# Correlation products on two 64-column tiles of the array, and a band of six image rows in place of eight

## The chip, the cores and the metric

The kernel runs on 1 core of one Trainium2 chip. The metric is the device time of one execution in microseconds (us), the median of several runs. The engines are named as in the profile: PE is TensorE's matmul (PEld its weight loads), DVE is VectorE, ACT is ScalarE, POOL is GpSimd, and SP is SyncE, which here only issues DMAs.

## What is computed

Two layers follow each other, each on 8 images of 512 channels and 32x32 pixels. A layer normalises the image by groups of channels, takes the 25 correlations of each pixel with its 5x5 neighbours over the channels (of vectors scaled to length one), puts these 25 beside the 512 channels, multiplies by a 512x537 matrix, adds a bias, clips at zero, and adds the result to the image.

```
norm = jnp.sqrt(jnp.sum(feature * feature, axis=1, keepdims=True))
fn = feature / jnp.maximum(norm, EPS)
fp = jnp.pad(fn, ((0, 0), (0, 0), (PAD, PAD), (PAD, PAD)))
for cc in range(CS):
    for r in range(CS):
        sims.append(jnp.sum(fp[:, :, r:h + r, cc:w + cc] * fn, axis=1))
...
out = jnp.einsum('bihw,oi->bohw', x, conv_w) + conv_b[None, :, None, None]
...
x = x + _L0_conv_ref(_gn(x), L0_conv_conv_w, L0_conv_conv_b)
x = x + _L1_conv_ref(_gn(x), L1_conv_conv_w, L1_conv_conv_b)
```

## The kernel before

**Units and slots.** One image of one layer is a unit; there are 16, numbered k = 0 to 15. The images stay in SBUF between the layers (a ring of five in `xs`). Each engine has its program written out by hand, and semaphores join them. From unit 3 on the programs run in slots, one for each unit: slot k begins when TensorE starts the correlation products of unit k. Behind them come eight groups of 12 or 13 large matmuls (`channels`, L530, and `volume`, L539) of the units k-2 and k-1. So a unit's correlations are made one slot before its large matmuls need them.

**The way of a unit's correlations.**

1. TensorE multiplies the normalised image with itself (`products`, L470). The weights are 4 image rows (128 pixels, all 128 columns of the array), and the 8 rows around them pass as 256 columns (192 at the upper and lower edge, where rows are missing). Four channel tiles and two precision parts make 8 matmuls for one block of 128 pixels, 64 in all. Two blocks share one PSUM bank. The sum of a pixel's products with its neighbours then lies in a band along the diagonal.
2. ScalarE copies each bank to SBUF, four times for a unit (`band_out_of_psum`, L643), and SP writes each copy to a DRAM scratch (`band_through_dram`, L340).
3. SP waits until all four have landed, and issues two reads (`skew<-band_dram`, L346). Their row step in DRAM is one element more than a row's length, so that each pixel's own neighbours land at the same place of every partition.
4. VectorE takes lengths and scales (`neighbours`, L832 to L852); ScalarE gives a square root in between (`lengths`, L648).
5. TensorE transposes the result (`turn`, L520), at group 6 of the eight. The groups 6 and 7 stand behind it in TensorE's program, and then the next unit's products.
6. ScalarE copies it out (L654), SP writes it to DRAM (`rows_to_dram`, L356 and L358), and GpSimd's queue reads seven shifted views of it (L267 to L277; in units 0 and 1 SP's queue does). VectorE makes the 25 correlations in the next slot (`correlation`), and GpSimd's queue puts them in place (L286) for `volume`.

**What waits in order.** Every engine works through its own program in order. On VectorE `neighbours` stands behind the additions of the groups 0 and 1, and before those of the groups 2 to 7 and the statistics of unit k+2. On ScalarE `lengths` stands before the clipping of group 2. On SP the writes of results (`tiles_out`, L323) stand around the band's, and in the slots 6 to 8 the loads of the next images (`tiles_in`, L331) follow, before `rows_to_dram`. `gram_ps` has two banks, `conv_ps` four, `act_out` two buffers.

Of the kernel before, what the change touches and what calls it, by code (L numbers as in the profile page):

```python
# [25 lines left out]
ACT = mybir.ActivationFunctionType  # L26
# [5 lines left out]
P = 128  # L32
HALF = 512
# [24 lines left out]
def build(nc, x, w0, b0, w1, b1, out):  # L58
# [10 lines left out]
    BAND = (ROWS + 2 * R) * WI  # L69
# [23 lines left out]
    GSZ = GPAD + BLOCKS * P * BAND + GPAD  # L93
    GROUPS = 2 * KT
    BN = 6
    assert (B, UNITS) == (BATCHES, B * LAYERS) and BAND * 2 == HALF
# [7 lines left out]
    with ctx:  # L104
# [22 lines left out]
        band = sb("band", [P, PAIRS, HALF], F32)  # L127
# [76 lines left out]
        CONSTS = 11  # L204
# [95 lines left out]
        def _(sp):  # L300
# [9 lines left out]
            def pads():  # L310
                sp.wait_ge(const_step, CONSTS)
                for q in range(2):
                    sp.dma_start(band_dram[q:q + 1, 0:GPAD], rows[0:1, 0:GPAD]).then_inc(pads_out, 16)
                    sp.dma_start(band_dram[q:q + 1, GSZ - GPAD:GSZ], rows[0:1, 0:GPAD]).then_inc(pads_out, 16)
# [18 lines left out]
            def band_through_dram(k):  # L333

                q = k % 2
                for p in range(PAIRS):
                    sp.wait_ge(band_sb, PAIRS * k + p + 1)
                    dst = bass.AP(band_dram, q * GSZ + GPAD + 2 * p * P * BAND,
                                  [[BAND, P], [P * BAND, 2], [1, BAND]])
                    sp.dma_start(dst, band[:, p, :].rearrange("p (a n) -> p a n", a=2)).then_inc(band_out, 16)  # L340
                sp.wait_ge(band_out, 16 * PAIRS * (k + 1))
                wait(sp, rn_step, RN_STEPS * k)
                for h in range(HALVES):
                    src = bass.AP(band_dram, q * GSZ + GPAD - R + h * FOLD * P * BAND,
                                  [[BAND + 1, P], [P * BAND, FOLD], [1, REACH]])
# [46 lines left out]
        def _(pool):  # L392
# [14 lines left out]
            pool.memset(band[:, 0, 0:R * WI], 0.0).then_inc(const_step, 1)  # L407
            pool.memset(band[:, PAIRS - 1, HALF - R * WI:HALF], 0.0).then_inc(const_step, 1)
# [44 lines left out]
        def _(pe):  # L453
# [10 lines left out]
            def product(u, j, t, part):  # L464

                p, h = j // 2, j % 2
                r0 = max(ROWS * j - R, 0)
                r1 = min(ROWS * (j + 1) + R, HI)
                at = h * BAND + (r0 - (ROWS * j - R)) * WI
                return pe.matmul(gram_at(u, p)[:, at:at + (r1 - r0) * WI],  # L470
                                 opnd[:, u % RING, 0, t, j * P:(j + 1) * P],
                                 opnd[:, u % RING, part, t, r0 * WI:r1 * WI],
                                 start=(t == 0 and part == 0 and (u > 0 or h == 0)),
                                 stop=(t == KT - 1 and part == 1 and (u > 0 or h == 1)))

            def first_products():

                for t in range(KT):
                    pe.wait_ge(high, t + 1)
                    pe.wait_ge(low, t + 1)  # L480
                    for p in range(PAIRS):
                        for j in (2 * p, 2 * p + 1):
# [507 lines left out]
```

## Time and profile before

| | |
|---|---|
| time, median of 3 runs | 539.54 us (538.83 to 540.25) |
| the profiled execution: span | 538.4 us |
| PE busy | 490.8 us, 91% of the span |
| DVE busy | 350.5 us, 65% |
| ACT busy | 278.6 us, 52% |
| chain that ended last | PE 77%, DVE 10%, ACT 4%, DMA 4% |

The page and the views give times in us from the span's start. Busy time counts an engine's instructions; matmuls follow each other in a pipeline, so one matmul's own duration is longer than the step to the next one, and steps are read from starting times. The span runs from the first to the last instruction of the profiled execution. It lies 1.1 us below the median of the runs.

### The profile page before, as it was taken

How to read it: one execution, taken by the hardware profiler on the slowest of the kernel's cores; microseconds unless marked ns; L12 is line 12 of the kernel's file. 1: busy time of each engine (PE TensorE's matmuls, PEld its weight loads, DVE VectorE, ACT ScalarE, POOL GpSimd, SP SyncE). 2: the span in 40 equal slices, each digit the busy share in tenths (PEclk: the TensorE clock that was granted, in tenths of full speed). 3: DMA queues.
4: the chain of work that ended last, by engine and by line, in shares of the span. 5: the costliest groups of instructions: out<-in, count | busy, mean ns of one | idle time of the engine just before them, and what ended most of it. 6: DMA issues, size and time to landing. Idle time of an engine off the chain costs nothing.

```text
span 538.4 us, 7705 instructions
## 1 busy us (share of the span) xinstructions
PE 490.8 (91%) x2824; PEld 278.2 (52%) x2824; DVE 350.5 (65%) x820; ACT 278.6 (52%) x370; POOL 131.8 (24%) x189
## 2 busy tenths in 40 slices
PE   0658699489998999999999999999999999999996
PEld 0535355354644646464645556464646455564442
DVE  4788794767869296958758595858677676433322
ACT  1352544575394656647393757556473938433222
POOL 3453511040521313131220404040313112040400
PEclk9989799789999999999999999999999999999999
DMA  8282444441332716494957625042332326362332
GB/s 295 99 270 67 129 165 133 133 134 38 94 92 74 219 49 211 149 309 131 321 165 254 212 102 161 15 129 47 98 89 75 110 79 185 138 203 90 126 126 114
DMA packets 58547, 75.81 MB, mean 141 GB/s; under 512 B 11764, under 2 KB 45612, under 8 KB 58510
## 3 DMA queue, kind: packets, MB, share of 16 engines
q1 hardware_dynamic: 48718, 66.40, 36.7%
q0 software_dynamic: 9792, 8.92, 7.0%
q8 instruction: 22, 0.36, 0.3%
q14 instruction: 15, 0.12, 0.1%
HBM read 34.97 MB, written 37.79 MB: 135 GB/s over the span
## 4 chain that ended last, share of the span: by engine, by line
PE 77%; DVE 10%; ACT 4%; DMA 4%; POOL 2%; SPq 2%; issue 2%; DVEq 0%; ACTq 0%
PE conv_ps L530 56%; PE gram_ps L470 14%; PE conv_ps L539 5%; DVE stats L759 3%; POOL v L432 2%; DVE opnd L808 2%; DMA xs<-in_x_dram 1%; ACT opnd L627 1%; PE turn_ps L520 1%; ACT v L633 1%; DVE wmax L858 1%; ACT act_out L662 1%; DMA skew<-band_dram 1%; DMA band_dram<-band 1%; DVE xs L886 1%
## 5 line engine op out<-in xcount | busy, mean ns | idle before, releaser
L530 PE MATMUL conv_ps<-opnd,wh 128*128 128x512 f16 x512 | 194.9, 381 | 1.2 <-DVE wl L874 1.2
L530 PE MATMUL conv_ps<-opnd,whh 128*128 128x512 f16 x512 | 194.7, 380 | 0.0
L530 PE MATMUL conv_ps<-opnd,wl 128*128 128x512 f16 x512 | 194.7, 380 | 0.0
L662 ACT ACTIVATE act_out<-conv_ps,bias,wdown 128x512 f32<-128x512 f32 x128 | 96.4, 775 | 141.0 <-PE conv_ps L539 129.1
L886 DVE TENSOR_TENSOR xs<-xs,act_out 128x512 f32<-128x512 f32 x128 | 87.7, 696 | 50.8 <-ACT act_out L662 50.2
L470 PE MATMUL gram_ps<-opnd 128*128 128x256 f16 (+1 forms) x960 | 105.0, 269 | 3.4 <-ACT band L643 3.4
L470 PEld LDWEIGHTS gram_ps<-opnd 128*128 128x128 f16 x960 | 91.1, 100 | 16.6 <-ACT band L643 3.7
L808 DVE SCALAR_TENSOR_TENSOR opnd<-opnd,v 128x1024 f16<-128x1024 f16 x64 | 78.4, 1235 | 28.7 <-ACT v L633 21.3
L627 ACT ACTIVATE opnd<-xs,affine 128x1024 f16<-128x1024 f32 x64 | 78.8, 1238 | 17.4 <-DVE affine L802 17.4
L759 DVE BATCH_NORM_STATS2 stats<-xs 128x6 f32<-128x512 f32 x128 | 79.9, 681 | 5.6 <-DMA xs<-in_x_dram 5.6
L530 PEld LDWEIGHTS conv_ps<-opnd,whh 128*128 128x128 f16 x512 | 50.0, 98 | 61.2 <-issue 1.0
L530 PEld LDWEIGHTS conv_ps<-opnd,wh 128*128 128x128 f16 x512 | 50.2, 98 | 58.8 <-POOL whh L424 1.3
L530 PEld LDWEIGHTS conv_ps<-opnd,wl 128*128 128x128 f16 x512 | 50.2, 98 | 57.5 <-issue 0.8
L633 ACT ACTIVATE v<-xs,affine 128x1024 f32<-128x1024 f32 x52 | 64.4, 1238 | 6.1 <-DVE opnd L808 6.1
L267 POOL DMA_DIRECT2D mirror<-rows_dram x14 | 9.5, 678 | 232.0 <-DMA rows_dram<-rows 232.0
L286 POOL DMA_DIRECT2D vol<-corr_h x48 | 33.2, 697 | 105.7 <-DVE corr_h L825 105.6
L539 PE MATMUL conv_ps<-vol,wvol 96*128 96x512 f16 x128 | 47.2, 396 | 11.7 <-DMA vol<-corr_h 11.7
L643 ACT ACTIVATE band<-gram_ps 128x448 f32<-128x448 f32 (+1 forms) x60 | 32.5, 560 | 20.2 <-PE gram_ps L470 20.2
L817 DVE TENSOR_TENSOR mirror<-mirror,rn_own 100x256 f32<-100x256 f32 x16 | 6.8, 424 | 49.1 <-DMA rn_far<-rows_dram 49.1
L277 POOL DMA_DIRECT2D rn_far<-rows_dram x56 | 34.1, 744 | 0.0
L539 PEld LDWEIGHTS conv_ps<-vol,wvol 96*128 96x128 f16 x128 | 12.6, 100 | 27.6 <-DMA vol<-corr_h 12.3
L432 POOL TENSOR_SCALAR v<-xs,affine 128x1024 f32<-128x1024 f32 x12 | 21.7, 1817 | 18.5 <-DVE affine L802 11.8
(77 smaller groups left out, 238.6 us busy)
## 6 DMA issues: line engine op xcount, KB each, us to landing
xs<-in_x_dram SPq DMA_DIRECT2D x32, 512.0 KB, 6.4
band_dram<-band SPq DMA_DIRECT2D x64, 256.0 KB, 2.9
out_dram<-xs SPq DMA_DIRECT2D x32, 512.0 KB, 2.9
skew<-band_dram SPq DMA_DIRECT2D x32, 266.0 KB, 3.5
vol<-corr_h POOLq DMA_DIRECT2D x48, 50.0 KB, 2.7
rows_dram<-rows SPq DMA_DIRECT2D x32, 65.8 KB
rows_dram<-rows SPq DMA_DIRECT2D x32, 63.3 KB
mirror<-rows_dram POOLq DMA_DIRECT2D x14, 110.9 KB, 2.6
```

Of the source, the lines that this page charges most:

```text
L277: eng.dma_start(rn_far[c:QPARTS:QUARTERS, 0:run], bass.AP(rows_dram, rn_row + c * QRUN, [[1, S], [PW, S], [1, run]])).then_inc(arrived, 16)
L286: eng.dma_start(vol[at:at + NS, k % 2, :].rearrange("s (q n) -> s q n", q=QUARTERS), corr_h[:, part, :]).then_inc(vol_in, 16)
L470: return pe.matmul(gram_at(u, p)[:, at:at + (r1 - r0) * WI], opnd[:, u % RING, 0, t, j * P:(j + 1) * P], opnd[:, u % RING, part, t, r0 * W ...
L530: pe.matmul(conv_ps[:, g % 4, :], w[:, l, t, m * P:(m + 1) * P], opnd[:, u % RING, part, t, n * HALF:(n + 1) * HALF], start=(t == 0 and w ...
L539: pe.matmul(conv_ps[:, g % 4, :], wvol[0:96, l, m * P:(m + 1) * P], vol[0:96, u % 2, n * HALF:(n + 1) * HALF], start=False, stop=True).the ...
L627: act.activation(opnd[:, u % RING, 0, t, :], xs[:, ring_slot(unit_batch(u)), t, :], ACT.Identity, bias=affine[:, 0, 1, t:t + 1], scale=aff ...
L633: act.activation(v2[:, t % 2, :], xs[:, ring_slot(unit_batch(u)), t, :], ACT.Identity, bias=affine[:, 1, 1, t:t + 1], scale=affine[:, 1, 0 ...
L643: act.activation(band[:, p, a:z], gram_at(u, p)[:, a:z], ACT.Copy).then_inc(band_sb, 1)
L662: act.activation(act_out[:, g % 2, :], conv_ps[:, g % 4, :], ACT.Relu, bias=bias[:, l, m:m + 1], scale=wdown[:, l, m:m + 1]).then_inc(relu, 1)
L759: last = dve.bn_stats(stats[:, t, h, :], xs[:, ring_slot(b), t, h * HALF:(h + 1) * HALF])
L808: dve.scalar_tensor_tensor(out=opnd[:, u % RING, 1, t, :], in0=opnd[:, u % RING, 0, t, :], scalar=-2.0, in1=v2[:, t % 2, :], op0=ALU.mult, ...
L886: dve.tensor_tensor(xt, xt, act_out[:, g % 2, :], ALU.add).then_inc(x_sum, 1)
```

## The change

The weights of one correlation matmul become 2 image rows (64 pixels) in place of 4, and 6 rows pass (192 columns) in place of 8. A block of 128 pixels is now made by two such matmuls, one on the array's columns 0 to 63 and one on the columns 64 to 127, in turn: for each channel tile and part first one half (`s` = 0), then the other. At the image's upper and lower edge a matmul of 64 columns fills the places of rows that are missing (`filler`). A bank holds the blocks p and p+4 in place of 2p and 2p+1.

The band is 192 columns wide in place of 256. ScalarE copies 384 columns of each bank. The DMA to DRAM writes each tile of 64 pixels in one piece, with a gap of 64 elements between tiles, and its destination has three steps (2 tiles, 64 pixels, 384 elements) in place of (128 pixels, 2 blocks, 256 elements). The reads keep their size and take another start and step. The two fills of the band's edges with zeros on GpSimd go, and the gaps in DRAM are filled with zeros once.

```diff
--- before.py
+++ after.py
@@ -66,7 +66,11 @@
     GROUP = C // 32
     ROWS = P // WI
     BLOCKS = PIX // P
-    BAND = (ROWS + 2 * R) * WI
+    TROWS = 2
+    TILE = TROWS * WI
+    SPLIT = P // TILE
+    BAND = (TROWS + 2 * R) * WI
+    STEP = 2 * BAND + 1
     PAIRS = BLOCKS // 2
     REACH = 2 * R * WI + S
     CENTRE = R * WI + R
@@ -90,10 +94,10 @@
     A_PITCH = S * (B_PITCH + PW) - 1
     ROWS_SZ = (NS + 1) * PSZ + S * A_PITCH
     GPAD = 64
-    GSZ = GPAD + BLOCKS * P * BAND + GPAD
+    GSZ = GPAD + PAIRS * P * STEP
     GROUPS = 2 * KT
     BN = 6
-    assert (B, UNITS) == (BATCHES, B * LAYERS) and BAND * 2 == HALF
+    assert (B, UNITS) == (BATCHES, B * LAYERS) and BAND * 2 <= HALF and TILE <= GPAD
 
     weights = (w0, w1)
     biases = (b0, b1)
@@ -124,7 +128,7 @@
         wvol = sb("wvol", [P, LAYERS, C], F16)
         vol = sb("vol", [P, 2, PIX], F16)
         v2 = sb("v2", [P, 2, PIX], F32)
-        band = sb("band", [P, PAIRS, HALF], F32)
+        band = sb("band", [P, PAIRS, 2 * BAND], F32)
         skew = sb("skew", [P, BLOCKS, REACH], F32)
         nbr = sb("nbr", [P, BLOCKS, H_PART], F32)
         rows = sb("rows", [H_PART + NROWS, FRAME], F32)
@@ -201,7 +205,7 @@
         relu = sem("relu")
         x_sum = sem("x_sum")
 
-        CONSTS = 11
+        CONSTS = 9
         BN_STEPS = KT + KT + 2
         GN_STEPS = 11
         RN_STEPS = 8
@@ -311,7 +315,9 @@
                 sp.wait_ge(const_step, CONSTS)
                 for q in range(2):
                     sp.dma_start(band_dram[q:q + 1, 0:GPAD], rows[0:1, 0:GPAD]).then_inc(pads_out, 16)
-                    sp.dma_start(band_dram[q:q + 1, GSZ - GPAD:GSZ], rows[0:1, 0:GPAD]).then_inc(pads_out, 16)
+                    sp.dma_start(bass.AP(band_dram, q * GSZ + GPAD + TILE * 2 * BAND,
+                                         [[TILE * STEP, PAIRS * SPLIT], [1, TILE]]),
+                                 rows[0:PAIRS * SPLIT, 0:TILE]).then_inc(pads_out, 16)
                 sp.wait_ge(pads_out, 64)
 
             def tiles_out(u, tiles):
@@ -335,14 +341,14 @@
                 q = k % 2
                 for p in range(PAIRS):
                     sp.wait_ge(band_sb, PAIRS * k + p + 1)
-                    dst = bass.AP(band_dram, q * GSZ + GPAD + 2 * p * P * BAND,
-                                  [[BAND, P], [P * BAND, 2], [1, BAND]])
-                    sp.dma_start(dst, band[:, p, :].rearrange("p (a n) -> p a n", a=2)).then_inc(band_out, 16)
+                    dst = bass.AP(band_dram, q * GSZ + GPAD + p * P * STEP,
+                                  [[TILE * STEP, SPLIT], [2 * BAND, TILE], [1, 2 * BAND]])
+                    sp.dma_start(dst, band[:, p, :]).then_inc(band_out, 16)
                 sp.wait_ge(band_out, 16 * PAIRS * (k + 1))
                 wait(sp, rn_step, RN_STEPS * k)
                 for h in range(HALVES):
-                    src = bass.AP(band_dram, q * GSZ + GPAD - R + h * FOLD * P * BAND,
-                                  [[BAND + 1, P], [P * BAND, FOLD], [1, REACH]])
+                    src = bass.AP(band_dram, q * GSZ + GPAD - R + h * BAND,
+                                  [[STEP, P], [P * STEP, FOLD], [1, REACH]])
                     sp.dma_start(skew[:, h:BLOCKS:HALVES, :], src).then_inc(skew_in, 16)
 
             def rows_to_dram(k):
@@ -404,8 +410,6 @@
                                pattern=[[GROUP, P // GROUP], [0, GROUP]], channel_multiplier=-1
                                ).then_inc(const_step, 1)
             pool.memset(rows[:, :], 0.0).then_inc(const_step, 1)
-            pool.memset(band[:, 0, 0:R * WI], 0.0).then_inc(const_step, 1)
-            pool.memset(band[:, PAIRS - 1, HALF - R * WI:HALF], 0.0).then_inc(const_step, 1)
             pool.memset(vol[:, :, :], 0.0).then_inc(const_step, 1)
             pool.memset(wvol[:, :, :], 0.0).then_inc(const_step, 1)
             pool.memset(nbr[:, :, NROWS:H_PART], 0.0).then_inc(const_step, 1)
@@ -461,17 +465,39 @@
                 pe.matmul(turn_ps[:, 1, 0:2 * KT], avg[:, :], mv[:, :, :].rearrange("p t s -> p (t s)"),
                           start=True, stop=True).then_inc(group_avg, 1)
 
-            def product(u, j, t, part):
-
-                p, h = j // 2, j % 2
-                r0 = max(ROWS * j - R, 0)
-                r1 = min(ROWS * (j + 1) + R, HI)
-                at = h * BAND + (r0 - (ROWS * j - R)) * WI
-                return pe.matmul(gram_at(u, p)[:, at:at + (r1 - r0) * WI],
-                                 opnd[:, u % RING, 0, t, j * P:(j + 1) * P],
-                                 opnd[:, u % RING, part, t, r0 * WI:r1 * WI],
-                                 start=(t == 0 and part == 0 and (u > 0 or h == 0)),
-                                 stop=(t == KT - 1 and part == 1 and (u > 0 or h == 1)))
+            def off_image(j, s):
+
+                top = TROWS * (j * SPLIT + s) - R
+                return max(-top, 0) * WI, max(top + TROWS + 2 * R - HI, 0) * WI
+
+            def tile_at(u, j, s, first, size):
+
+                at = j // FOLD * BAND + first
+                return gram_at(u, j % FOLD)[s * TILE:(s + 1) * TILE, at:at + size]
+
+            def opens(u, j):
+
+                return u > 0 or j < FOLD
+
+            def filler(u, j, s):
+
+                above, below = off_image(j, s)
+                n, size = j * SPLIT + s, above + below
+                if size:
+                    pe.matmul(tile_at(u, j, s, 0 if above else BAND - below, size),
+                              opnd[:, u % RING, 0, 0, n * TILE:(n + 1) * TILE],
+                              opnd[:, u % RING, 0, 0, 0:size], start=opens(u, j), stop=False)
+
+            def product(u, j, s, t, part):
+
+                above, below = off_image(j, s)
+                n = j * SPLIT + s
+                first, size = (TROWS * n - R) * WI + above, BAND - above - below
+                return pe.matmul(tile_at(u, j, s, above, size),
+                                 opnd[:, u % RING, 0, t, n * TILE:(n + 1) * TILE],
+                                 opnd[:, u % RING, part, t, first:first + size],
+                                 start=(t == 0 and part == 0 and opens(u, j) and size == BAND),
+                                 stop=(t == KT - 1 and part == 1 and (u > 0 or j >= FOLD)))
 
             def first_products():
 
@@ -479,9 +505,13 @@
                     pe.wait_ge(high, t + 1)
                     pe.wait_ge(low, t + 1)
                     for p in range(PAIRS):
-                        for j in (2 * p, 2 * p + 1):
+                        for j in (p, p + FOLD):
+                            if t == 0:
+                                for s in range(SPLIT):
+                                    filler(0, j, s)
                             for part in range(2):
-                                last = product(0, j, t, part)
+                                for s in range(SPLIT):
+                                    last = product(0, j, s, t, part)
                         if t == KT - 1:
                             last.then_inc(gram, 1)
 
@@ -491,10 +521,13 @@
                     pe.wait_ge(high, KT * (u + 1))
                     pe.wait_ge(low, KT * (u + 1))
                 pe.wait_ge(band_sb, PAIRS * u + p - 1)
-                for j in (2 * p, 2 * p + 1):
+                for j in (p, p + FOLD):
+                    for s in range(SPLIT):
+                        filler(u, j, s)
                     for t in range(KT):
                         for part in range(2):
-                            last = product(u, j, t, part)
+                            for s in range(SPLIT):
+                                last = product(u, j, s, t, part)
                 last.then_inc(gram, 1)
 
             def turn_weights(l, n):
@@ -638,9 +671,7 @@
                 act.wait_ge(gram, PAIRS * u + p + 1)
                 if p == 0:
                     wait(act, band_out, 16 * PAIRS * u)
-                a = R * WI if p == 0 else 0
-                z = HALF - (R * WI if p == PAIRS - 1 else 0)
-                act.activation(band[:, p, a:z], gram_at(u, p)[:, a:z], ACT.Copy).then_inc(band_sb, 1)
+                act.activation(band[:, p, :], gram_at(u, p)[:, 0:2 * BAND], ACT.Copy).then_inc(band_sb, 1)
 
             def lengths(u):
```

On TensorE one half of the products of a unit from slot 3 on, and the beginning of the other, stand so before (`turn_ps<-mv,avg` is the group average of the next unit, in the middle of the products; the numbers behind a name are partitions and columns of the output):

```order
L470 MATMUL gram_ps<-opnd 128x192 x8
L470 MATMUL gram_ps<-opnd 128x256 x24
L461 MATMUL turn_ps<-mv,avg 128x8
L470 MATMUL gram_ps<-opnd 128x256 x24
L470 MATMUL gram_ps<-opnd 128x192 x8
```

And around the same average in the changed program, to the beginning of the last block (L487 is the filler):

```order
L496 MATMUL gram_ps<-opnd 64x128
L496 MATMUL gram_ps<-opnd 64x192 x49
L465 MATMUL turn_ps<-mv,avg 128x8
L496 MATMUL gram_ps<-opnd 64x192 x48
L487 MATMUL gram_ps<-opnd 64x64
L496 MATMUL gram_ps<-opnd 64x192
L496 MATMUL gram_ps<-opnd 64x128
```

Nothing has moved past the average; a unit has 128 products of half the weights' columns in place of 64, and two fillers.

On SP's queue the DMAs of unit 3 stand so before (the numbers are the steps' counts of the destination):

```order
L340 DMA band_dram<-band 128x2x256 x4
L346 DMA skew<-band_dram 128x4x133 x2
L356 DMA rows_dram<-rows 26x648
L358 DMA rows_dram<-rows 5x5x648
L356 DMA rows_dram<-rows 26x648
```

And in the changed program:

```order
L346 DMA band_dram<-band 2x64x384 x4
L352 DMA skew<-band_dram 128x4x133 x2
L362 DMA rows_dram<-rows 26x648
L364 DMA rows_dram<-rows 5x5x648
L362 DMA rows_dram<-rows 26x648
```

The order on SP is the same; the destination of the band's writes has 2 as its outermost count in place of 128.

## Rows read from the trace of the kernel before

**Rows 1.** The page: span, and busy time of each engine.
```profile
span 538.4 us, 7705 instructions
...
PE 490.8 (91%) x2824; PEld 278.2 (52%) x2824; DVE 350.5 (65%) x820; ACT 278.6 (52%) x370; POOL 131.8 (24%) x189
```

**Rows 2.** TensorE in slot 12, in order of time: start, duration, line.
```profile
381.48 3.44 PE L470 MATMUL gram_ps<-opnd 128*128 128x192 f16 x32
384.75 0.29 PE L461 MATMUL turn_ps<-mv,avg 128*128 128x8 f32 x2
...
405.03 0.60 PE L520 MATMUL turn_ps<-ident,nbr 128*115 128x128 f32 x4
...
411.09 1.15 PE L470 MATMUL gram_ps<-opnd 128*128 128x192 f16 x11
```

**Rows 3.** Line 470 alone, slot 12, eight matmuls: busy PE, PEld.
```profile
381.48:382.13 0.65, 0.65 (x8) 0.65 (x8) 1.00 0.00 0
```

**Rows 4.** SP's queue in slot 12, in order of time: issue, time it took, line.
```profile
383.78 6.38 SPq L340 DMA_DIRECT2D band_dram<-band  x4
392.19 0.92 SPq L346 DMA_DIRECT2D skew<-band_dram  x2
```

**Rows 5.** VectorE in slot 12, in order of time.
```profile
397.86 0.17 DVE L832 TENSOR_SCALAR nsq<-skew 128x8 f32<-128x8 f32 x1
...
400.13 0.91 DVE L852 TENSOR_TENSOR nbr<-skew,nbr 128x200 f32<-128x200 f32 x2
```

**Rows 6.** DMA issues by line, with median us to landing.
```profile
band_dram<-band SPq DMA_DIRECT2D x64, 256.0 KB, 2.9
...
skew<-band_dram SPq DMA_DIRECT2D x32, 266.0 KB, 3.5
```

**Rows 7.** DMA packets from 390.0 to 392.1: two band DMAs.
```profile
DMA packets 544, 0.52 MB, mean 250 GB/s; under 512 B 32, under 2 KB 544, under 8 KB 544
...
q1 hardware_dynamic: 544, 0.52, 73.0%
```

**Rows 8.** DMA packets from 380.2 to 381.7: one DMA of line 358.
```profile
DMA packets 31, 0.08 MB, mean 54 GB/s; under 512 B 5, under 2 KB 5, under 8 KB 30
...
q1 hardware_dynamic: 30, 0.06, 12.9%
```

**Rows 9.** DMA packets from 49 to 52: lines 267 to 277 on SP's queue.
```profile
q1 hardware_dynamic: 261, 0.29, 30.8%
...
rn_far<-rows_dram SPq DMA_DIRECT2D x4, 27.7 KB
```

**Rows 10.** DMA queues from 384.0 to 388.6: the views beside the band.
```profile
q0 software_dynamic: 364, 0.39, 37.3%
```

**Rows 11.** SP's queue in slots 7 and 8: loads of x, then the band.
```profile
255.72 2.91 SPq L331 DMA_DIRECT2D xs<-in_x_dram  x4
...
265.32 7.11 SPq L340 DMA_DIRECT2D band_dram<-band  x4
```

**Rows 12.** SP's queue in unit 0, in order of time.
```profile
26.88 1.98 SPq L340 DMA_DIRECT2D band_dram<-band  x4
31.35 0.91 SPq L346 DMA_DIRECT2D skew<-band_dram  x2
```

**Rows 13.** VectorE in unit 0, in order of time.
```profile
40.91 0.89 DVE L852 TENSOR_TENSOR nbr<-skew,nbr 128x200 f32<-128x200 f32 x2
```

**Rows 14.** TensorE, first products of slots 3, 4 and 5.
```profile
104.37 3.78 PE L470 MATMUL gram_ps<-opnd 128*128 128x192 f16 x32
...
138.46 3.44 PE L470 MATMUL gram_ps<-opnd 128*128 128x192 f16 x32
...
173.90 0.34 PE L470 MATMUL gram_ps<-opnd 128*128 128x192 f16 x2
```

**Rows 15.** Stretches: busy time, granted clock (PEclk), DMA share, GB/s.
```profile
56.90:61.70 4.80, 0.13 (x2) 0.04 (x1) 2.82 (x13) 2.36 (x4) 4.18 (x5) 0.89 0.31 87
61.80:65.20 3.40, 3.40 (x9) 1.16 (x10) 2.46 (x3) 2.78 (x4) 3.11 (x2) 0.50 0.29 89
```

## The prediction

> **What bounds the kernel now.** I began with the page: TensorE is busy for 490.8 of 538.4 us [rows 1], so a saving elsewhere gives nothing as long as nothing makes TensorE wait. Then I read one slot in order of time on each engine. Slot 12 takes 411.09 - 381.48 = 29.61 us [rows 2], without a gap on TensorE: 6.7 us of products, 16.9 us of groups 0 to 5, the turn at 405.03, which is 23.55 us after the slot's start (I write +23.55), and 6.06 us from there to the next slot. The reader is to see that the turn is the only place in a slot where TensorE depends on work of the same slot: the way products, copy, band to DRAM, skew, neighbours, turn. That way has slack. SP issues the first band write at +2.30 and the skew reads at +10.71 [rows 4]; neighbours ends at 401.04, +19.56 [rows 5], 4.0 us before the turn. The first operation on the skew starts at 397.86, +16.38; the reads, issued within 0.92 us and landing in 3.5 us [rows 4, 6], are there at about +14.5, so VectorE came 1.9 us later than it might have. All in all the band may land some 5.9 us later before TensorE waits.
>
> **The products.** Of the first 32, eight pass 192 columns at 81 ns each [rows 3]; the other 24 fill the rest of 3.27 us [rows 2], 109 ns each. The trace has no matmul on half of the array. If the two halves run side by side, a pair costs one passage of 192 columns, 81 ns: 64 pairs make 5.2 us, with fillers and changes between whole and half array perhaps 5.4, a gain of 1.3 us a slot. If they run one behind the other, a pair costs 162 ns and the products 10.4 us, a loss of 3.7 us. If weight loads were not covered either, a load of about 81 ns, the second figure of [rows 3], on each gives 324 ns a pair and 20.7 us. I take the middle of the first two, no difference in the products' length, because the term that follows hides both ends: TensorE reaches the turn at +22.3 or +27.3, and either is too early. The end of the first quarter, which starts the band, moves by -0.3 to +1.0 us; I take 0.
>
> The Trainium skill, TensorEngine Tiling (Array Packing), section Theoretical Speedup, gives up to 2x for such tiles, but its section Restrictions says that column tiling turns the fast weight load off. By the first the products would take about 5.2 us and by the second the loads could be seen; no run here shows either yet.
>
> **The band's write to DRAM** is the term that I think decides. Its destination's outermost count was 128 and is now 2. The trace shows what that count does. Each DMA ends with one small packet on every engine that it used, and these are the packets under 512 B: two band writes of 128 leave 32, so 16 engines each [rows 7]; a DMA of line 358, with 5 outermost in DRAM, leaves 5 [rows 8]. The views on SP's queue, 25 outermost on their DRAM side or 5, keep 30.8% of 16 engines busy, 4.9 engines, and this although several of them are in the queue at once [rows 9]: DMAs behind each other use the same five, they do not take others. So I expect each band write on two engines, and all four of a unit on the same two.
>
> The Trainium skill, DMA: Bandwidth & Descriptors, section Why a DMA increments its semaphore by 16 and not by 1, states it as a rule: the largest number up to 16 that divides the outermost counts of both sides, on the lowest-numbered engines. The rows above agree (16 for 128, 5 for 5 and 25); by the rule the count here is 2.
>
> Price of a packet: 73.0% of 16 engines for 2.1 us over 512 packets of 1 KB is 48 ns [rows 7]; 12.9% for 1.5 us over 25 packets of 2592 B is 124 ns [rows 8]. Both are 47 to 48 ns per KB; the new packets of 1536 B come to 72 ns. These rows were taken with busy engines beside them, so I use 68 (bounds 60 and 80). One engine carries 64 packets of each write: 4.35 us, and 17.4 us for four (15.4 to 20.5). The copies come fast enough to keep the two busy. Before, a write of 256 KB took 2.9 us to landing [rows 6], of which 256 packets on 16 engines are 0.8, so 2.1 us are fixed.
>
> New way in a slot: first issue +2.3, fixed part and transfers 2.1 + 17.4, landed at +21.8 (was +10.7); skew reads 3.8, +25.6; neighbours 2.5 without its wait for VectorE, +28.1. The views on GpSimd's queue run at the same time; they use 37.3% of 16 engines for 4.6 us [rows 10], 1.7 us on a mean engine, and I add 1.0 for what falls on the two. So the turn comes at +29.1, not at +23.55: 5.5 us later (2.5 to 9).
>
> **The clock.** TensorE then waits about 5.6 us at each turn. In unit 0's wait before, 4.8 us nearly without matmuls were followed by 3.4 us at a granted 0.50, the level of 1.2 GHz [rows 15]. The 6.06 us behind a turn would run at that level for some part; I add 1.5 us (0 to 3.4). Together 7.0 us a slot. If the products run one behind the other, TensorE comes at +27.3, waits less and keeps its clock, but the band starts 1.0 us later: the sum stays about the same.
>
> **Which slots.** Slots 5 to 15 are eleven: 77 us. Slots 3 and 4 already take 34.1 and 35.4 us [rows 14], because second-layer weights are turned in them, and the new way needs 29.1 + 6.06 = 35.2: nothing more. In unit 0 the first write is issued at 26.88 and the skew at 31.35 [rows 12]; now the band lands at 26.88 + 19.5 = 46.4, the reads at 50.2, neighbours ends at 52.7 in place of 41.80 [rows 13]: 10.9 us, and TensorE has little to do meanwhile. Units 1 and 2 have more slack; 2 us each. Start: 15 us (10 to 22). In slots 7 to 9 the band's first write stands behind loads of x issued by the slot before (four of 512 KB [rows 11], 128 KB on each engine, some 6 us); SP now issues these loads later in the slot, since it waits for the band first, so they reach into the next. I add 2.7 us three times, 8 us (0 to 15).
>
> **Small edits.** ScalarE's copy of 384 columns in place of 512 and the two fills less on GpSimd shorten work that is not waited for: 0. The bytes to DRAM fall by a quarter, which would matter if 16 engines carried them. The skew reads keep their shape, 128 outermost: 0.
>
> **Sum.** 538.4 + 77 + 15 + 8 = 638.4 us of span; with the 1.1 us by which the median lies above the span, 639.5, so 640 us.
>
> **Rivals.**
> Faster: the write spreads over 16 engines after all, as every DMA of 128 partitions shows [rows 7], and the halves run side by side. Then the band lands no later than now, and 15 units gain 1.3 us each (unit 0 waits for its input): 520 us. Against it stand the five engines of [rows 8, 9]. What decides the sign then is a pair of products at 102 ns, the mean of 16 steps of 81 and 48 of 109 now.
> Slower, but otherwise: 16 engines, and the halves one behind the other: 15 x 3.7 = 56 us, 595 us.
> Two engines, but other two for each write: the last one lands about 3.6 us later than now, within the slack of 5.9, and the products decide: 520 or 595.
> Much slower: weight loads uncovered. A slot then takes 20.7 + 16.9 + 6.06 = 43.7 us, 14 more in 15 units: about 750 us.
>
> **Chances.** My forecast (two engines, band late at every turn) 0.82; spread and side by side 0.08; spread and serial 0.06; loads uncovered 0.04. Its own range adds the low bounds, 3 x 11 + 10 = 43 us, and the high ones within reason, 11 x 10.5 + 22 + 15 = 152 us: 582 to 692. I give 588 to 690, which holds most of it and the 595 case, some 8 in 10. A measurement of this kernel can tell about 0.3% from no change. Faster by more than that 0.07, within it 0.02, slower 0.91.
>
> **What would show it.** In the profile after: band writes with 4 packets under 512 B for two of them in place of 32; landing of the band, where it is told, several times 2.9 us; SP waiting for the band before the skew for some 14 us in a slot; TensorE idle before line 553, put down to VectorE's `nbr`; DMA share near 2/16 in the middle of a quiet slot; clock at 0.5 behind the turns. A pair of products at 81 or 162 ns shows the array's part. I am wrong if the band lands at its old place, if a turn starts at +24 or earlier, or if the packets take well under 60 ns.

## The result, and the profile after

The changed kernel takes 671.93 us (median of four runs, 670.90 to 672.83), the kernel before 539.89 us (four runs, 538.83 to 540.68). The ratio is 1.2451, with a 95% interval of 1.2428 to 1.2474: slower by almost a quarter. The profiled execution has a span of 671.0 us, 132.6 us more than before.

The page of the changed kernel: span, busy time, the chain of waits by engine and by line, and two groups of instructions with the idle time ahead of them.

```profile
span 671.0 us, 9815 instructions
...
PE 521.6 (78%) x3880; PEld 284.5 (42%) x3880; DVE 349.5 (52%) x820; ACT 274.0 (41%) x370; POOL 128.6 (19%) x187
...
DMA 43%; PE 30%; DVE 14%; ACT 5%; issue 4%; SPq 2%; POOL 1%; DVEq 0%; ACTq 0%
DMA band_dram<-band 34%; PE conv_ps L563 19%; DMA skew<-band_dram 8%; PE gram_ps L496 6%; DVE stats L790 3%; PE turn_ps L553 2%; ACT band L674 2%; ACT opnd L660 1%; DVE nbr L883 1%; SPq L346 1%; DVE xs L917 1%; PE conv_ps L572 1%; DVE opnd L839 1%; SPq L352 1%; DMA xs<-in_x_dram 1%
...
L553 PE MATMUL turn_ps<-ident,nbr 128*115 128x128 f32 x64 | 18.1, 434 | 90.6 <-DVE nbr L883 90.6
...
L863 DVE TENSOR_SCALAR nsq<-skew 128x8 f32<-128x8 f32 x16 | 2.8, 172 | 151.0 <-DMA skew<-band_dram 151.0
```

TensorE is busy 78% of the span in place of 91% [rows 1]. The chain now runs through DMAs for 43% of the time, 34% in the band's writes alone, and 90.6 us of TensorE's idle time stand ahead of one line, the turn. What makes the turn late is seen in slot 12, the slot that [rows 2, 4, 5] show of before. TensorE, in order of time:

```profile
483.27 2.83 PE L496 MATMUL gram_ps<-opnd 128*64 128x192 f16 x64
486.03 0.39 PE L465 MATMUL turn_ps<-mv,avg 128*128 128x8 f32 x2
486.35 2.47 PE L496 MATMUL gram_ps<-opnd 128*64 128x192 f16 x49
...
489.33 0.39 PE L563 MATMUL conv_ps<-opnd,wh 128*128 128x512 f16 x1
...
511.64 1.20 PE L553 MATMUL turn_ps<-ident,nbr 128*115 128x128 f32 x4 [5.28 <-DVE nbr L883]
520.15 0.22 PE L487 MATMUL gram_ps<-opnd 128*64 128x64 f16 x1
```

SP's queue in the same slot:

```profile
485.33 8.47 SPq L346 DMA_DIRECT2D band_dram<-band  x4
505.34 0.95 SPq L352 DMA_DIRECT2D skew<-band_dram  x2
```

And VectorE in that slot:

```profile
509.19 0.17 DVE L863 TENSOR_SCALAR nsq<-skew 128x8 f32<-128x8 f32 x1 [9.66 <-DMA skew<-band_dram]
...
510.69 0.90 DVE L883 TENSOR_TENSOR nbr<-skew,nbr 128x200 f32<-128x200 f32 x2
```

The products got shorter: from the slot's start to the average, 64 of them take 2.76 us where the first 32 of before took 3.27. The first band write is issued at +2.06 (before +2.30). Then SP waits, and the skew reads go out at +22.07, not +10.71; VectorE stands idle 9.66 us for them; neighbours ends at 511.59, +28.32; the turn comes at +28.37 after 5.28 us of waiting. From there to the next slot it is 8.51 us, before 6.06.

Why the band is late is in the DMA packets. From 493 to 497, when nothing but band writes is under way:

```profile
DMA packets 132, 0.20 MB, mean 50 GB/s; under 512 B 2, under 2 KB 132, under 8 KB 132
...
q1 hardware_dynamic: 132, 0.20, 13.2%
```

2 of 16 engines are 12.5%: two are busy and fourteen idle. 13.2% of 16 x 4 us over the 130 packets that are not small is 65 ns a packet of 1536 B. One write ended in this stretch and left two packets under 512 B, where 16 engines left 16 a write [rows 7].

The clock behind the turn of the same slot, as a whole and in its two parts (columns as in [rows 15]):

```profile
511.64:520.15 8.51, 8.51 (x30) 3.87 (x30) 8.51 (x14) 2.71 (x4) 0.28 (x1) 0.73 0.12 33
...
511.64:516.28 4.64, 4.64 (x13) 2.30 (x14) 4.64 (x8) 1.94 (x3) 0.00 (x0) 0.50 0.02 6
516.28:520.15 3.87, 3.87 (x18) 1.57 (x16) 3.87 (x8) 0.78 (x1) 0.28 (x1) 1.00 0.23 66
```

The whole stretch has the same work as the 6.06 us of before, at a mean granted clock of 0.73, after 5.28 us in which TensorE had nothing to do: 4.64 us at 0.50, the level of 1.2 GHz, and the rest at 1.00, that of 2.4 GHz.

The 132.6 us lie in three places, each measured by the first products of a slot. Slot 3 starts at 129.31 in place of 104.37 [rows 14]: 24.9 us. Slots 3 and 4 together take 17.9 us more (slot 5 starts at 216.69, before 173.90: 42.8 us, less 24.9). Slots 5 to 15, with the groups that follow the last of them, take the rest, 89.8 us. TensorE's first products of unit 2 and its turn, the first products of slot 3 and its turn, and those of slot 5:

```profile
90.66 5.33 PE L496 MATMUL gram_ps<-opnd 128*64 128x192 f16 x64
...
125.40 1.20 PE L553 MATMUL turn_ps<-ident,nbr 128*115 128x128 f32 x4 [7.19 <-DVE nbr L883]
129.31 5.07 PE L496 MATMUL gram_ps<-opnd 128*64 128x192 f16 x64
...
163.03 1.20 PE L553 MATMUL turn_ps<-ident,nbr 128*115 128x128 f32 x4 [4.17 <-DVE nbr L883]
...
216.69 0.22 PE L487 MATMUL gram_ps<-opnd 128*64 128x64 f16 x1
```

SP's first band write in units 2 and 3:

```profile
100.12 7.43 SPq L346 DMA_DIRECT2D band_dram<-band  x4
...
137.43 7.73 SPq L346 DMA_DIRECT2D band_dram<-band  x4
```

Slot 4 shows another wait than the turn's, here on TensorE:

```profile
193.99 0.38 PE L563 MATMUL conv_ps<-opnd,whh 128*128 128x512 f16 x1
203.38 0.87 PE L543 MATMUL gram_ps<-ident,xs 128*128 128x128 f32 x3 [9.01 <-DVE wl L905]
```

and on VectorE:

```profile
197.78 0.17 DVE L863 TENSOR_SCALAR nsq<-skew 128x8 f32<-128x8 f32 x1 [7.70 <-DMA skew<-band_dram]
...
202.56 0.68 DVE L905 TENSOR_TENSOR wl<-gram_ps,wh 128x512 f16<-128x512 f32 x1
```

The low parts of the second layer's weights (line 905) stand on VectorE behind the first operation on the skew. When the skew is late, they are late too, and TensorE's transposes of the next weights wait for them.

### The profile page after: what moved, and what is told of

Its sections match the earlier page's. It is cut to its first block, busy times and chain, and to the rows that moved or that the text cites. A ratio compares the mean times of both kernels' runs of the same rounds, so it can differ in the third digit from the quotient of the medians.

```text
span 671.0 us, 9815 instructions
## 1 busy us (share of the span) xinstructions
PE 521.6 (78%) x3880; PEld 284.5 (42%) x3880; DVE 349.5 (52%) x820; ACT 274.0 (41%) x370; POOL 128.6 (19%) x187
## 4 chain that ended last, share of the span: by engine, by line
DMA 43%; PE 30%; DVE 14%; ACT 5%; issue 4%; SPq 2%; POOL 1%; DVEq 0%; ACTq 0%
DMA band_dram<-band 34%; PE conv_ps L563 19%; DMA skew<-band_dram 8%; PE gram_ps L496 6%; DVE stats L790 3%; PE turn_ps L553 2%; ACT band L674 2%; ACT opnd L660 1%; DVE nbr L883 1%; SPq L346 1%; DVE xs L917 1%; PE conv_ps L572 1%; DVE opnd L839 1%; SPq L352 1%; DMA xs<-in_x_dram 1%
## 5 line engine op out<-in xcount | busy, mean ns | idle before, releaser
L563 PE MATMUL conv_ps<-opnd,wh 128*128 128x512 f16 x512 | 207.2, 405 | 1.4 <-ACT act_out L693 1.0
L563 PE MATMUL conv_ps<-opnd,wl 128*128 128x512 f16 x512 | 205.9, 402 | 0.0
L563 PE MATMUL conv_ps<-opnd,whh 128*128 128x512 f16 x512 | 204.5, 399 | 0.0
L496 PE MATMUL gram_ps<-opnd 128*64 128x192 f16 (+1 forms) x1920 | 92.7, 254 | 4.2 <-ACT band L674 3.8
L553 PE MATMUL turn_ps<-ident,nbr 128*115 128x128 f32 x64 | 18.1, 434 | 90.6 <-DVE nbr L883 90.6
L496 PEld LDWEIGHTS gram_ps<-opnd 128*64 128x64 f16 x1920 | 84.1, 115 | 7.2 <-ACT band L674 6.9
L563 PEld LDWEIGHTS conv_ps<-opnd,wh 128*128 128x128 f16 x512 | 53.0, 103 | 67.7 <-issue 12.0
L863 DVE TENSOR_SCALAR nsq<-skew 128x8 f32<-128x8 f32 x16 | 2.8, 172 | 151.0 <-DMA skew<-band_dram 151.0
L679 ACT ACTIVATE nrm<-nsq 128x8 f32<-128x8 f32 x16 | 3.3, 208 | 148.7 <-DVE nsq L863 148.7
L572 PE MATMUL conv_ps<-vol,wvol 96*128 96x512 f16 x128 | 47.3, 396 | 11.4 <-DMA vol<-corr_h 11.4
L553 PEld LDWEIGHTS turn_ps<-ident,nbr 128*115 128x115 f32 x64 | 13.4, 288 | 98.4 <-DVE nbr L883 98.4
```

The costliest lines, as they stand in the source:

```text
L496: return pe.matmul(tile_at(u, j, s, above, size), opnd[:, u % RING, 0, t, n * TILE:(n + 1) * TILE], opnd[:, u % RING, part, t, first:first ...
L553: last = pe.transpose(turn_ps[0:H_PART + NROWS, 0, i * P:(i + 1) * P], both[:, i, 0:H_PART + NROWS], ident[:, :])
L563: pe.matmul(conv_ps[:, g % 4, :], w[:, l, t, m * P:(m + 1) * P], opnd[:, u % RING, part, t, n * HALF:(n + 1) * HALF], start=(t == 0 and w ...
L572: pe.matmul(conv_ps[:, g % 4, :], wvol[0:96, l, m * P:(m + 1) * P], vol[0:96, u % 2, n * HALF:(n + 1) * HALF], start=False, stop=True).the ...
```

## Experiments

The theory after the result: the outermost count of the band write's destination puts the write on two engines, and all the loss follows from that. Rivals: the loss comes from the products on half the array, from the new layout in DRAM, or from the clock. The kernels with two writes a bank and with one row step ran four to six times; each of the others ran once. Runs of one kernel lie up to 4 us apart here, so a difference of 3 to 4 us between single runs is weak evidence.

**Two writes a bank.** The same layout and products; only the outermost count becomes 64.

```diff
-dst = bass.AP(band_dram, q*GSZ + GPAD + p*P*STEP, [[TILE*STEP, SPLIT], [2*BAND, TILE], [1, 2*BAND]])
-sp.dma_start(dst, band[:, p, :])
+for s in range(SPLIT):
+    dst = bass.AP(band_dram, q*GSZ + GPAD + (p*P + s*TILE)*STEP, [[2*BAND, TILE], [1, 2*BAND]])
+    sp.dma_start(dst, band[s*TILE:(s + 1)*TILE, p, :])
```

> The changed kernel, but each bank's copy is written to DRAM by two DMAs, one for each tile of 64 pixels, so that 64 stands outermost and not 2; products, band and reads are those of the change. Theory (two DMA engines carry the band's writes, and that is the whole loss): the band lands where it did before the change, no wait at the turn, clock at 1.0 in the steady slots, and the products keep their gain of 0.6 us in each of 15 units: 528 to 534 us. Rival (the half-array products or the new reads cost time themselves): 550 to 672 us.

Measured: 535.76 us, ratio to before 0.9936 (0.9914 to 0.9959). All of the loss is gone, and the products show a gain. SP's queue in its slot 12, which starts at 379.52:

```profile
381.59 7.58 SPq L347 DMA_DIRECT2D band_dram<-band  x8
391.10 0.95 SPq L353 DMA_DIRECT2D skew<-band_dram  x2
```

TensorE in that slot, the turn and the next slot's start:

```profile
402.45 0.60 PE L554 MATMUL turn_ps<-ident,nbr 128*115 128x128 f32 x4
408.61 0.60 PE L497 MATMUL gram_ps<-opnd 128*64 128x192 f16 x12
```

Skew at +11.57, turn at +22.93 without a wait, slot 29.08 us in place of 29.61. It is 4 us faster than before, somewhat less than I had expected: slots 3 and 5 give some of it back (35.58 and 30.08 us, before 34.09 and 29.62); why is open.

**Before's products, written to DRAM with an outermost count of 2.** The kernel before with rows of 512 in DRAM, once with a gap of 64 elements after 64 rows, which keeps the two dimensions apart, once without it, where they are one dimension of 128. Both read the skew in four pieces.

```diff
+SIDE = P // 2 * HALF + GAP      # GAP = 64 in the first, 0 in the second
-dst = bass.AP(band_dram, ..., [[BAND, P], [P * BAND, 2], [1, BAND]])
+dst = bass.AP(band_dram, ..., [[SIDE, 2], [HALF, P // 2], [1, HALF]])
```

The first:

> The kernel before, products on the whole array, but both blocks of a bank in one row of 512 elements in DRAM, with a gap of 64 elements between the halves of 64 pixels, and four reads in place of two. The write's outermost count is 2. Theory: 64 packets of 2 KB on each of two engines, 5.4 us a write and 21.5 us for four; the turn comes at about +32, TensorE waits there in each slot, 700 to 750 us. Rival (the loss belongs to the half-array products): 535 to 550 us.

The second:

> As the run with the gap, with a gap of 0, so that the write's outermost count is 128; everything else is the same, four reads too. Theory: 16 engines, 536 to 545 us. Rival (the new order of blocks or the four reads cost the time): as the run with the gap, above 650 us.

Measured: 770.96 us with the gap, 540.61 without it (540.15 for the kernel before beside them). TensorE's instructions are the same in both. The packets of the second from 390.5 to 392.6, two writes:

```profile
DMA packets 288, 0.52 MB, mean 250 GB/s; under 512 B 32, under 2 KB 32, under 8 KB 288
```

These are 16 small packets a write, as before. The packets of the first from 568 to 572:

```profile
DMA packets 100, 0.20 MB, mean 51 GB/s; under 512 B 0, under 2 KB 0, under 8 KB 100
...
q1 hardware_dynamic: 100, 0.20, 13.1%
```

Its turn in slot 12:

```profile
591.52 1.20 PE L524 MATMUL turn_ps<-ident,nbr 128*115 128x128 f32 x4 [10.13 <-DVE nbr L856]
```

Again two engines, 84 ns for a packet of 2 KB, and a wait of 10.13 us. The loss is above the 700 to 750 us that I had expected; slots 8 to 14 take 41.5 to 44.9 us, where before they took 29.6. So the outermost count, without any change on TensorE, makes the loss; the layout and the four reads cost nothing. The gap itself is not to blame either: the kernel with two writes a bank has one after each 64 rows.

**TensorE kept busy before the turn.** 18 matmuls whose result nobody reads, ahead of the turn in slots 3 and 5 to 15, to take the clock's share by itself.

```diff
 def turn(u):
+    if u >= STEADY and u != W1_SLOT:
+        pe.wait_ge(band_sb, PAIRS * (u + 1))
+        for i in range(WARM):                       # 18
+            pe.matmul(gram_ps[:, 0, :], wh[:, 0, 0, 0:P], opnd[:, u % RING, 0, 0, 0:HALF], start=True, stop=True)
```

> The changed kernel with 18 matmuls of 512 columns that nothing uses ahead of each turn in the slots 3 and 5 to 15, some 3.9 us of work in a wait of 4.2 to 8 us. Theory (some 3 us of each slot's loss are the clock that falls in the wait): granted clock near 1.0 behind the turn, groups 6 and 7 in 5.6 us again, 25 to 36 us less than the changed kernel, 636 to 647 us. Rival (the groups behind the turn are slow for another reason, or the extra matmuls come in the way): 670 us or more.

Measured: 668.38 us, so I had expected far too much. In quiet slots the clock did stay up. Slot 12 from the turn to its end:

```profile
510.39:516.63 6.24, 6.24 (x31) 2.96 (x31) 6.24 (x10) 2.72 (x4) 0.00 (x0) 1.00 0.11 31
```

That is 8.51 - 6.24 = 2.3 us less. But the next turn comes later: slots 10 to 13 together went from 145.6 to 140.1 us, 1.4 us a slot where 2.4 had been gained behind the turn on the mean, and their turns came at +28.5 to +29.0 in place of +27.3 to +28.4. The hardware queue's packets from 1.5 to 5.5 us after the start of slot 12, in the changed kernel:

```profile
q1 hardware_dynamic: 28, 0.04, 5.2%
```

and in this one:

```profile
q1 hardware_dynamic: 11, 0.02, 1.1%
```

The band's packets start later here, at +4.49 in place of +3.47. As the slot's end is shorter, the transfers of the unit before (the rows to DRAM and the views of them) fall into the beginning of the next slot, ahead of the band; that order is read from the trace and not tested by itself. In slots 6 to 9, 14 and 15 the 18 matmuls ended 3 to 4 us before the turn, and the clock fell all the same; slots 6 and 14 even grew by 2.7 and 1.6 us, since SP issued their first band write at +4.36 and +4.35, not at +2.07. So the clock's time is a real cost, but the way of the band through DRAM, which decides when the next turn comes, takes about two fifths of a gain there back.

**Neighbours later on VectorE.** `NORM_AT = 2` becomes 4 in the changed kernel.

> The changed kernel, with the lengths' and neighbours' steps of VectorE put two steps later in the slot (the number that places them 4 in place of 2). Theory: in slot 4 the low parts of the second layer's weights stand on VectorE behind the neighbours, which now end at +28.7, and TensorE waits 9.0 us for them; with the neighbours placed later, the low parts come before them, slot 4 is 9 us shorter or nearly so, and the other slots stay as they are, since the turn's wait ends with the skew's landing either way: 655 to 665 us. Rival: slot 4 is long for the band's landing as every slot is, and the order on VectorE changes nothing: 670 to 674 us. If the statistics or the scaled weights that now come ahead of the neighbours delay these in every slot, more than 675 us.

Measured: 656.14 us, 15.8 us less and inside the expected range, but only half of it comes from where the theory had it. In slot 4 TensorE now waits at the turn alone (first row: transposes of weights):

```profile
197.53 0.60 PE L543 MATMUL gram_ps<-ident,xs 128*128 128x128 f32 x4
200.41 0.69 PE L553 MATMUL turn_ps<-ident,nbr 128*115 128x128 f32 x4 [2.27 <-DVE nbr L883]
```

Slot 4 takes 37.25 us in place of 44.93, 7.7 us less. Slots 5 to 9, which the theory had left as they are, gave 6.7 us more, 3.9 of them in slots 7 to 9. There the loads of x go out sooner, here those issued in slot 6, first in the changed kernel and then in this one:

```profile
287.85 2.88 SPq L337 DMA_DIRECT2D xs<-in_x_dram  x4
```

```profile
270.06 5.47 SPq L337 DMA_DIRECT2D xs<-in_x_dram  x4
```

That is 6.4 and 13.6 us ahead of slot 7, so fewer packets of loads and results stand before the next band, whose last packet starts at +21.8 and not at +23.3. This is read from the traces and not tested by itself; slot 5's 2.3 us stay open.

**The halves' products apart.** All eight products of one half of the columns ahead of the other half's eight, in two kernels.

```diff
-for t in range(KT):
-    for part in range(2):
-        for s in range(SPLIT):
+for s in range(SPLIT):
+    for t in range(KT):
+        for part in range(2):
             last = product(u, j, s, t, part)
```

In the kernel with two writes a bank:

> The kernel with two writes a bank (535.8 us), with all eight products of one half of the columns ahead of all eight of the other half, so that two products that follow each other use the same half of the array. Theory: products on different halves run beside each other (a pair in 86 ns), and apart one follows the other (81 ns each): the 128 products of a slot take 9.2 to 10.4 us in place of 5.5, TensorE waits for nothing at the turn, so a slot goes from 29.1 to 32.8 or 34 us, and the run to 580 to 600 us. Rival: the halves do not run beside each other at all, a product of 192 columns simply takes 43 ns with its weights, and the order is of no account: 534 to 540 us.

In the changed kernel:

> The same order of products in the changed kernel (671.9 us). Theory of the prediction: the products' length is hidden, since TensorE waits 4 to 8 us at the turn anyway; what is left is that the first bank is full 1 to 1.2 us later and all writes, the skew reads and the turn with it: 675 to 690 us, with the wait at the turn 3 to 4 us shorter. Rival: TensorE's time counts in full, 4 us or more a slot: 720 us or more.

Measured: 544.64 us for the first. A slot takes 29.83 us, 0.75 more, not 4 to 5. My theory, that products must alternate between the halves to run beside each other, falls; the rival, that order is of no account, is nearer, but its reason (no overlap at all) was still to be tried. The products of slot 7, which starts at 236.79:

```profile
236.84 3.24 PE L497 MATMUL gram_ps<-opnd 128*64 128x128 f16 x64
...
240.33 2.78 PE L497 MATMUL gram_ps<-opnd 128*64 128x192 f16 x51
...
243.60 0.39 PE L564 MATMUL conv_ps<-opnd,wh 128*128 128x512 f16 x1
...
266.62 0.22 PE L488 MATMUL gram_ps<-opnd 128*64 128x64 f16 x1
```

The trace also shows that starts do not keep the program's order: the first product on the second half starts 0.285 us after the slot's start, while the last three of the first half's eight, which stand ahead of it in the program, start at 0.335 to 0.447 us.

The changed kernel with the same order took 675.52 us, 3.6 more, where the kernel with two writes a bank lost 8.9 by it. So the products' length is for the most part hidden behind the turn's wait, as the prediction had it; the test is a small one, since the products grew by 0.75 us a slot and not by the 3 to 4 that I had reckoned with, and slot 12's wait shrank by 1 us (4.31 in place of 5.28).

**One half alone.** The kernel with two writes a bank, which leaves out the other half's products from slot 6 on.

```diff
-for s in range(SPLIT):
+for s in range(SPLIT if u < STEADY + 3 else 1):     # products and fillers
```

> The kernel with two writes a bank (535.8 us), which from slot 6 on leaves out the products on the second half of the columns (64 of the 128 products of a slot; the lower 64 rows of the band then hold old numbers). Theory: the two halves run beside each other, each product of 192 columns holding its half for 82 ns, so that half the products take as long as all of them: the products from the slot's start to the first convolution take 5.5 to 6.1 us as before, the slot stays 28.6 to 29.1 us, the run 530 to 537 us. Rival: a product takes 43 ns and the halves do not overlap; then the products take 3.2 to 3.5 us, and each of ten slots is 2.6 to 2.9 us shorter, since the neighbours have 4 us in hand before the turn: 506 to 512 us.

Measured: 534.97 us; a slot 28.89 us, against 29.08 with all products. The products of slot 9:

```profile
292.94 0.22 PE L488 MATMUL gram_ps<-opnd 128*64 128x64 f16 x1
292.99 2.59 PE L497 MATMUL gram_ps<-opnd 128*64 128x128 f16 x32
...
295.83 3.05 PE L497 MATMUL gram_ps<-opnd 128*64 128x192 f16 x32
298.81 0.39 PE L565 MATMUL conv_ps<-opnd,wh 128*128 128x512 f16 x1
```

Half the products take 298.81 - 292.94 = 5.87 us, all of them 6.06. On the one half, full products follow each other by 82 to 83 ns. So the two halves run beside each other, and together with the run before, also where eight products of one half stand in a row.

**One row step.** The changed products, with rows of 384 at one step in DRAM: one write of 128 rows a bank, four skew reads. Then the same with `NORM_AT = 4`.

```diff
-dst = bass.AP(band_dram, ..., [[TILE * STEP, SPLIT], [2 * BAND, TILE], [1, 2 * BAND]])
+dst = bass.AP(band_dram, ..., [[2 * BAND, P], [1, 2 * BAND]])
-src = bass.AP(band_dram, ..., [[STEP, P], [P * STEP, FOLD], [1, REACH]])
+for s in range(SPLIT):
+    src = bass.AP(band_dram, ... + s * TILE * 2 * BAND, [[STEP, TILE], [P * 2 * BAND, FOLD], [1, REACH]])
```

> The changed kernel's products, with rows of 384 in DRAM all at one step, so that each bank is one write of 128 rows (outermost count 128 in place of 2), and each half of the skew read as two reads of 64 partitions (four reads in place of two). Theory: only the count of the outermost dimension of the write matters, 16 engines carry each write, the skew is issued near +11.3, TensorE waits for nothing at the turn and a slot is 29.1 us as with two writes a bank; with four writes fewer a slot SP issues sooner at the start: 530 to 538 us. Rival: the time went with the new layout or the 64-row pieces of the skew, and stays over 580 us.

> The kernel with one row step (534.4 us) with the lengths' and neighbours' steps two steps later in the slot (4 in place of 2), as was done to the changed kernel, where it gave 15.8 us. Theory: there the gain came from slots 4 and 5, where work for the next unit stood behind late neighbours; with the skew early, slots 4 and 5 have 2.0 us (low parts of the weights) and some 3 us to give, and the neighbours' 4 us in hand before the turn pay for the delay in the others: 528 to 534 us. Rival: the delay of the lengths and neighbours uses up more than the 4 us in hand, and TensorE waits at the turn in every slot: 538 us or more.

Measured: 534.39 us, ratio to before 0.9892 (0.9875 to 0.9909), and 533.34 us, 0.9887 (0.9857 to 0.9917). Both beat both kernels; between the two no difference can be told, so what the later place is worth here is not shown. SP's queue in slot 11 of the first, which starts at 352.18:

```profile
354.24 6.00 SPq L344 DMA_DIRECT2D band_dram<-band  x4
361.85 2.61 SPq L351 DMA_DIRECT2D skew<-band_dram  x4
```

The skew goes out at +9.67, earlier than with eight writes. The four reads cost SP 2.61 us of issuing, but neighbours still ends 4 us ahead of the turn. Slots 4 and 5 take longer here than before (36.86 and 33.62 us, before 35.44 and 29.62); why is open.

## Why the prediction was right

The forecast was 640 us, in a range of 588 to 690; measured were 671.9. The mechanism held step by step. Two terms of the sum were far too small, the start and slots 3 and 4; in slots 5 to 15 two misses nearly cancel.

**The band's write on two engines** was right and nearly rightly sized: 65 ns a packet where I had taken 68, skew issued at +22.07 where I had the landing at +21.8, neighbours done at +28.32 for +28.1. The turns of slots 5 to 15 came at +29.1 on the mean, the figure that I had for a slot without loads of x. Such slots, 10 to 13, had theirs at +27.3 to +28.4, about 1.3 us sooner than forecast; slots 7 to 9, where the loads of x stand before the band, had them at +30.2 to +31.1. The Trainium skill, DMA: Bandwidth & Descriptors, section Why a DMA increments its semaphore by 16 and not by 1, has the rule (the largest number up to 16 that divides the outermost counts). The two kernels with rows of 512 agree: with an outermost count of 2 the write keeps 13.1% of 16 engines busy.

**The clock** I had put at 1.5 us a slot. Behind the turn it takes 2.6 on the mean of slots 5 to 14 (8.70 us against 6.06). Where the extra matmuls kept it up, in slots 10 to 13, the slots got 1.4 us shorter for 2.4 us gained behind the turn. By these four slots the term is near what I had put, but by luck, since two misses cancel: too little behind the turn, and nothing for the next band that starts later.

**Slots 5 to 15** took 89.8 us more; I had 77 for them and 8 for the loads of x. Of the 89.8, the later turns make 60.8 (5.5 us each), where I had 5.5 each and the loads' 8 besides; the stretches behind the turns make 26.5 and what follows the last turn 2.5, where I had 16.5 for the clock. The sum is near because the first miss pays for part of the second.

**Slots 3 and 4** I had put at nothing more; they took 17.9 us. The step that failed is "the new way needs 29.1 + 6.06 = 35.2", which sets the band's first issue at +2.3 there too. In slot 3 of the changed kernel SP issues it at +8.12, and at the prediction's own prices that gives a turn at 8.1 + 19.5 + 3.8 + 2.5 = +33.9 (measured +33.72). In slot 4 I did not look at what stands on VectorE behind the neighbours: the weights' low parts, 9.0 us, which placing the neighbours later took away.

**The start** I had put at 15 us, with "units 1 and 2 have more slack; 2 us each"; it took 24.9. Unit 0's 10.9 was right (unit 1's first products start at 60.86, before 50.16), and unit 1 took 2.8. The failed step is the same in unit 2: its first band write goes out at 100.12, +9.46, so the same sum gives +35.3, where its turn had stood at +26.4 before: 8.9 us, not 2. Measured are +34.7 and a wait of 7.2 us; the unit took 11.4 us more.

**The products' length** I had left between 5.4 and 10.4 us, hidden either way. Side by side was right: 6.06 us in place of 6.70. The 6.70 is read in slot 12 of the kernel before, from its start in [rows 2] to the first large matmul, the second row here:

```profile
384.90 3.44 PE L470 MATMUL gram_ps<-opnd 128*128 128x256 f16 x32
388.17 0.38 PE L530 MATMUL conv_ps<-opnd,wh 128*128 128x512 f16 x1
```

The Trainium skill, TensorEngine Tiling (Array Packing), section Theoretical Speedup, gives up to 2x; the run with one half alone agrees that the second half of the products is all but free (5.87 against 6.06 us). Weight loads do not show in the length. The gain over before is 0.64 us and not the 1.3 that I had for this case. The price of a full pair was right, 82 to 83 ns by the steps on each half, but with the filler and the two halves' running apart before the average, 32 pairs take 2.76 us, 86 ns each, and the average between the products takes 0.32 us in place of 0.15. Hidden it was for the most part: products 0.75 us longer in every slot cost 3.6 us in the one run.

## What to carry to other kernels

Look at the outermost count of a DMA's destination before and after a change of layout: here 2 in place of 128 cost 132 us, and a layout with one row step, or two writes of 64 rows, turned the same change into a gain of 0.6 to 1.1%. When a way becomes longer than its slack, put its price to each slot with that slot's own issue times, and follow what stands in the queues behind the operation that waits; the terms that I set to little or nothing without doing so were the furthest off. What a loop gains at one place is not its gain in the run when another way, here the band through DRAM, sets when the next step can come.

## What the runs showed of the hardware that I had not expected

Two engines wrote packets of 1536 B in 65 ns and of 2048 B in 84 ns, 41 to 42 ns per 1000 B, where the packets of 1024 B among 16 busy engines had taken 48 ns [rows 7], 47 ns per 1000 B.

The two column halves run beside each other without strict alternation: with eight products of one half in a row, 128 products take 6.81 us with the average (slot 29.83 against 29.08), where one half's 64 alone take 5.87, with the average too. In that run, products on one half start ahead of products on the other that stand before them in the program.

In one run, 18 matmuls before the turn kept the clock at 1.00 where they left TensorE idle for 0.9 to 1.6 us ahead of it (slots 5 and 10 to 13); where they left 3.2 to 4.2 us, it fell (mean 0.72 to 0.81 behind the turn).
